# Four graph layers on one core: the last step and the tail in another order on TensorE, DVE and ACT

## The chip, the cores and the metric

The kernel runs on one core of a Trainium2 chip. The metric is the time of one execution in device microseconds, the median of several executions. The engines are named as in the profile: PE (TensorE, matmuls and transposes), DVE (VectorE), ACT (ScalarE), POOL (GpSimd) and SP (here only the queue of the loads and stores). Each engine works through its own list of instructions in order, and engines wait for each other by semaphores.

## The reference

The input is x, 32 graphs of 256 nodes with 128 features, and an adjacency matrix of 256 by 256. Four layers follow each other, each with a residual and a layer norm without weights over the 128 features:

```
x = layernorm(x + L0(x))   # A_hat x, Linear 128->256, batchnorm, relu, Linear 256->128, batchnorm
x = layernorm(x + L1(x))   # attention over 256 edges, 4 heads, softmax by source node, Linear
x = layernorm(x + L2(x))   # three layers S = adj*adj: relu(S x W1), relu(S h W2), S h W3 (128->256->512->128)
x = layernorm(x + L3(x))   # dense attention:
#   Wh = x W;  e = leaky_relu(Wh a1 + (Wh a2)^T);  e = -inf where adj == 0
#   L3 = softmax(e) Wh
```

Only the layers 2 and 3 are at work in the stretch that is changed.

## The kernel before

The 32 graphs are worked on in pairs, a pair is a **slot** (s = 0 or 1), and two slots are a **step** (p = 0 to 7, since `IT` is 8). The layers run as a pipeline over steps: while TensorE has layer 2 of step p in hand, layer 3 of step p - 2 and p - 1 is under way. All orders are written out by hand: each engine has a list of calls to small helper functions, and the order of these calls is the order of the work. There is no scheduler.

The names of the last steps are `K = IT - 3` (5), `M = IT - 2` (6) and `L = IT - 1` (7). When layer 2 of step L is being finished, layer 3 of K is finished beside it, and layer 3 of M and L is left for the tail. In the tail a piece of layer 3 is one slot and is numbered u: u = 0 and 1 are the slots of M, u = 2 and 3 those of L; j is the graph within the slot.

Layer 2 of step L, slot s, on its last stretch:

- `hidden2(L, s, g)` (PE, L1804): one of the four 128-row parts g of the projection to 512, as three matmuls for each product (a high and a low half of the numbers, L238 to L240). ACT applies the relu, `relu1` (L1541) for slot 1.
- `narrow(L, s)` (PE, L1811): the projection from 512 to 128. ACT rounds it, `s3_high` (L1402), DVE takes the rest, `s3_low` (L897), both out of PSUM.
- `mix_out(L, s)` (PE, L1822): the last product with the weighted adjacency. It needs `s3_low`.
- `add(L, s, ...)` (DVE, L875) adds the residual; `end_norm_stats(s)` (DVE, L1052), `end_power(s)` (POOL, L599) and `end_norm(s)` (DVE, L1065) are the layer norm behind it.

Layer 3 of a slot:

- `slot_scores(p, s, c, ...)` (DVE, L1044): Wh a1 or Wh a2 of four blocks of 128 nodes, c says which. c = 1 is what PE needs for `end_spread_scores(s)` (L1982), which lays the scores over the partitions.
- `end_maxima(s)` (DVE, L1074), `end_sums(s)` (ACT, L1492), `end_highest(s)` (DVE, L1082), `end_leaky(s)` (DVE, L1093), `end_exps(s)` (ACT, L1499): masked maximum, sum of both scores, leaky relu and exponential, in `soft`, which both steps M and L use. So L can't write slot s of `soft` before PE has turned the exponentials of M (`exr_done`, L1198 and L1209).
- `end_turn(u, s, j, base)` (PE, L1957), `end_copied` (ACT, L1509), `end_attend` (PE, L1965), `end_attended` (ACT, L1517), `end_output` (PE, L1974), `end_add` (DVE, L1100): transpose of the exponentials, the product with x, the product with W, division by the sum and residual.
- the norms that end layer 3: for K `ln_stats`, `ln_var_eps` (DVE, L178 and L192), `ln_power` (POOL, L200), `ln_scale` (ACT, L228) on the tile `ob`; for M the same for both slots at once, with slot 0 applied by DVE (`ln_apply`, L220) and slot 1 by ACT; for L by `fin_norm_stats`, `fin_power` and `fin_norm` (L1111, L604, L1125), a graph pair j at a time. SP stores K when `ln3.done` allows it, then graph by graph L slot 0, M, and L slot 1 (L398 to L407).

## Time and profile before

| | us |
|---|---|
| median of 3 runs | 585.36 |
| lowest and highest | 584.73 and 586.92 |
| the profiled execution | 586.41 |
| its span (first to last instruction) | 584.6 |
| PE, DVE, ACT, POOL busy | 537.5, 423.2, 370.3, 210.5 |
| mean granted share of TensorE's clock | 0.96 |

The span is what the instructions of the profiled execution cover, and 1.8 us lie around it. In a row of the timeline the first number is the start, the second how long the merged row lasts, and what stands in brackets is the idle time ahead of it and whose result ended it. The change touches only what starts after 534 us; the code up to there is the same.

### The profile page before, as it was taken

The numbers are of one execution on the slowest core, as the hardware profiler recorded it, in microseconds if no ns is written. First come the engines' busy times: TensorE is split into PE (matmuls) and PEld (weight loads), VectorE is DVE, ScalarE is ACT, GpSimd is POOL, SyncE is SP. The second block draws the span as 40 slices with busy tenths as digits, with TensorE's granted clock in tenths as the row PEclk, the third lists the DMA queues.
The fourth block names the chain that finished last, engine by engine and source line by source line (L and its number), as shares of the span: only waits on it lengthen the run. The fifth ranks groups of instructions, "written<-read, shape, count | busy, mean of one in ns | idle before, by whom it ended". The sixth has DMA issues, their size and how long they took to land.

```text
span 584.6 us, 11192 instructions
## 1 busy us (share of the span) xinstructions
PE 537.5 (92%) x3482; PEld 468.7 (80%) x3482; DVE 423.2 (72%) x1454; ACT 370.3 (63%) x741; POOL 210.5 (36%) x248
## 2 busy tenths in 40 slices
PE   3999799589999879999999999999999999999872
PEld 3888433468887679898998998998998998989762
DVE  4688667778986165358879679679778776787887
ACT  3666692557755414536568768778678677675682
POOL 8830530457575240501813513514514314310103
PEclk9999799689999769999999999999999999999997
DMA  7223000221200000000000100100100100100012
GB/s 229 72 79 101 2 0 0 72 74 44 64 0 1 0 2 1 1 0 2 2 1 2 36 0 1 36 0 0 36 0 0 36 1 0 38 0 1 2 37 73
DMA packets 28383, 15.26 MB, mean 26 GB/s; under 512 B 2320, under 2 KB 28048, under 8 KB 28352
## 3 DMA queue, kind: packets, MB, share of 16 engines
q1 hardware_dynamic: 27792, 13.65, 8.1%
q0 software_dynamic: 560, 1.25, 0.6%
q8 instruction: 14, 0.23, 0.2%
q14 instruction: 17, 0.14, 0.1%
HBM read 10.69 MB, written 4.19 MB: 25 GB/s over the span
## 4 chain that ended last, share of the span: by engine, by line
PE 79%; DVE 12%; ACT 4%; issue 2%; POOL 2%; DMA 0%; DVEq 0%; POOLq 0%; ACTq 0%; SPq 0%
PE psum L238 15%; PE psum L240 14%; PE psum L239 14%; PE psum L1818 9%; PE psum L1643 6%; PE psum L1685 5%; PE psum L1760 2%; PE psum L1770 2%; PE psum L1692 2%; PE psum L1696 2%; PE psum L1706 2%; DVE ln_st L184 2%; PE psum L1864 2%; PE psum L1846 2%; POOL ln_r L203 1%
## 5 line engine op out<-in xcount | busy, mean ns | idle before, releaser
L203 POOL TENSOR_TENSOR ln_r<-ln_v,mhalf 128x8 f32<-128x8 f32 x30 | 50.0, 1666 | 238.9 <-DVE ln_v L197 238.9
L1818 PE MATMUL psum<-l2w_s,h 128*128 128x128 f32 x512 | 59.8, 275 | 0.0
L1818 PEld LDWEIGHTS psum<-l2w_s,h 128*128 128x128 f32 x512 | 59.0, 192 | 0.8
L238 PE MATMUL psum<-qt_hi,l2w_s_hi 128*128 128x512 f32 x128 | 52.7, 412 | 0.0
L240 PE MATMUL psum<-qt_hi,l2w_s_lo 128*128 128x512 f32 x128 | 50.7, 396 | 0.0
L239 PE MATMUL psum<-qt_lo,l2w_s_hi 128*128 128x512 f32 x128 | 50.6, 395 | 0.0
L232 ACT ACTIVATE keep_x<-keep_x,ln_b,ln_r (+1 forms) x108 | 44.4, 487 | 7.0 <-DVE keep_x L224 4.4
L1400 ACT ACTIVATE h<-psum 128x512 f32<-128x512 f32 x60 | 34.8, 593 | 11.7 <-PE psum L240 11.6
L184 DVE BATCH_NORM_STATS2 ln_st<-keep_x 128x6 f32<-128x128 f32 (+1 forms) x192 | 39.4, 278 | 2.9 <-ACT keep_x L1328 1.6
L238 PE MATMUL psum<-wgt_hi,h_hi 128*128 128x256 f32 x128 | 37.1, 290 | 0.9 <-DVE h_lo L888 0.9
L240 PE MATMUL psum<-wgt_hi,h_lo 128*128 128x256 f32 x128 | 35.8, 280 | 0.0
L239 PE MATMUL psum<-wgt_lo,h_hi 128*128 128x256 f32 x128 | 35.7, 279 | 0.0
L1643 PE MATMUL psum<-hraw,w2t 128*128 (+1 forms) x64 | 32.1, 655 | 3.6 <-ACT hraw L1292 3.6
L1685 PE MATMUL psum<-sel,x1s_hi 128*128 128x512 f32 x64 | 27.6, 431 | 5.8 <-POOL x1s_lo L511 3.2
L888 DVE SCALAR_TENSOR_TENSOR h_lo<-psum,h_hi 128x1024 fp32r<-128x1024 f32 x16 | 19.6, 1225 | 16.2 <-ACT h_hi L1391 16.2
L1643 PEld LDWEIGHTS psum<-hraw,w2t 128*128 128x128 f32 x64 | 12.1, 207 | 22.9 <-issue 18.2
L911 DVE SCALAR_TENSOR_TENSOR soft<-keep_x,wa 128x128 f32<-128x128 f32 x96 | 30.0, 381 | 0.0
L899 DVE TENSOR_TENSOR s_lo<-psum,s_hi 128x512 fp32r<-128x512 f32 x16 | 11.1, 692 | 25.7 <-ACT s_hi L1404 25.7
L240 PEld LDWEIGHTS psum<-qt_hi,l2w_s_lo 128*128 128x128 f32 x128 | 24.1, 188 | 5.8
L1396 ACT ACTIVATE qt_hi<-psum 128x1024 fp32r<-128x1024 f32 x16 | 16.4, 1024 | 19.2 <-PE psum L240 19.2
L895 DVE TENSOR_TENSOR qt_lo<-psum,qt_hi 128x1024 fp32r<-128x1024 f32 x16 | 19.6, 1223 | 12.0 <-ACT qt_hi L1396 12.0
L239 PEld LDWEIGHTS psum<-qt_lo,l2w_s_hi 128*128 128x128 f32 x128 | 24.2, 189 | 4.4
(268 smaller groups left out, 1764.7 us busy)
## 6 DMA issues: line engine op xcount, KB each, us to landing
xin<-in_x SPq DMA_DIRECT2D x64, 128.0 KB, 2.3
out_x<-ob SPq DMA_DIRECT2D x24, 128.0 KB, 1.8
out_x<-keep_x SPq DMA_DIRECT2D x8, 128.0 KB, 1.9
l2w_raw<-in_l2w POOLq DMA_DIRECT2D x1, 512.0 KB, 5.1
adjs<-in_adj SPq DMA_DIRECT2D x1, 256.0 KB, 2.7
adjs<-in_adj_t SPq DMA_DIRECT2D x1, 256.0 KB, 2.9
l2w_s<-in_l2w POOLq DMA_DIRECT2D x1, 256.0 KB, 4.9
w_raw<-in_w_t SPq DMA_DIRECT2D x1, 128.0 KB, 2.8
```

Source lines behind the costliest of these rows:

```text
L184: i = dve.bn_stats(ln.st[:, s, k, :], y(s, k // 2, k % 2))
L203: pool.tensor_tensor(ln.r[:].rearrange("p s k -> p (s k)"), ln.v[:].rearrange("p s k -> p (s k)"), mhalf[:], ALU.pow).then_inc(ln.root, 1)
L232: i = act.activation(y(s, k // 2, k % 2), y(s, k // 2, k % 2), ACT.Identity, bias=ln.b[:, s, k:k + 1], scale=ln.r[:, s, k:k + 1])
L238: pe.matmul(o, lhs[0], rhs[0], start=start, stop=False)
L239: pe.matmul(o, lhs[0], rhs[1], start=False, stop=False)
L240: return pe.matmul(o, lhs[1], rhs[0], start=False, stop=stop)
L888: dve.scalar_tensor_tensor(out=h1[1][:, s].rearrange("p j t f -> p (j t f)"), in0=bank(2 * s, 2).rearrange("p k c -> p (k c)"), scalar=0.0 ...
L911: i = dve.scalar_tensor_tensor(out=soft[:, s, k, c * D:(c + 1) * D], in0=xn[:, q, k // 2, k % 2, :], scalar=1.0, in1=wa[:, c, :], op0=ALU. ...
L1400: act.activation(h2[:, s, g, :], bank(4 + g)[:, 0, :], ACT.Relu).then_inc(h2_out, 1)
L1643: i = pe.matmul(bank(s)[:, 0, :], w2t[:, k, :], hraw[:, k, q, :], start=(k == 0), stop=(k == 1))
L1685: i = pe.matmul(gathered_bank(s)[:, j, :], x1s[h][:, s, t, j, :], sel[:, t].rearrange("p k e -> p (k e)"), start=(n == 0), stop=(n == 3))
L1818: i = pe.matmul(bank(s)[:, 0, k * D:(k + 1) * D], h2[:, s, g, j * N + t * P:j * N + (t + 1) * P], l2w3_s[:, g, :], start=(g == 0), stop=(g ...
```

## The change

On **PE**, in the last step, the turn order becomes: `attend3(K, 1)`, `narrow(L, 0)`, `output3(K, 1)`, then both last projections to 512, `hidden2(L, 1, 0)` and `hidden2(L, 1, 1)`, then `mix_out(L, 0)` and `narrow(L, 1)`. The transposes of both slots of M stand behind `narrow(L, 1)`, and `mix_out(L, 1)` follows. In the tail the exponentials of L are turned later: slot 0's behind the outputs of M, and slot 1's in two halves around the product of slot 0.

On **DVE**, `s3_low(L, 0)` moves behind `slot_sum3(K, 1)`, the statistics of K are taken slot by slot, `s3_low(L, 1)` moves ahead of the scores of L's slot 0, and `add(L, 1)` with its norm moves ahead of `end_maxima(0)`. The norm of M is taken by slots (`end_norm_stats(2 + s)`), each behind that slot's additions, and DVE applies none of it.

On **ACT**, `s3_high(L, 0)` moves behind the exponentials of M's slot 0, the scaling of K's slots moves from between `end_copied(2, j)` and `end_sums(1)` to both sides of `s3_high(L, 1)`, the exponentials of L are split by halves, and both slots of M are scaled at the end.

On **POOL**, one power of eight numbers for M becomes two of four, each with its product.

```diff
@@ POOL
+            def sixth_shift(s):
+                pool.wait_ge(ln0.rstd, IT + 2 + s + 1)
+                pool.tensor_tensor(ln0.b[:, s], ln0.m[:, s], ln0.r[:, s], ALU.mult).then_inc(ln0.root, 1)
...
-            ln_power(pool, IT - 2, ln3)
+            for s in range(2):
+                end_power(2 + s)
+                sixth_shift(s)
@@ DVE
-            def end_norm_stats(s):
-                dve.wait_ge(ln2.added, 2 * L + s + 1)
+            def end_norm_stats(n):
+                s = n % 2
+                q = 2 * L + s if n < 2 else 2 * M + s
...
+                if n >= 2:
+                    dve.tensor_scalar(ln0.m[:, s], ln0.ag[:, s, :, 0], -1.0, None, ALU.mult)
...
-            s3_low(L, 0)
+            fifth_stats(0)
             leaky3(M, 1)
             slot_sum3(K, 1)
-            ln_stats(dve, last_sum, K, ln3)
+            s3_low(L, 0)
+            fifth_stats(1)
+            fifth_moments()
             ln_var_eps(dve, K, ln3)
             add(L, 0, o2_done, 2, ln2)
             end_norm_stats(0)
             weights3(M, False)
             end_norm(0)
+            s3_low(L, 1)
 
             dve.wait_ge(exr_done, 2 * M + 2)
             slot_scores(L, 0, 1, s12_ok)
-            s3_low(L, 1)
             slot_scores(L, 0, 0, own_ok)
-            end_maxima(0)
             add(L, 1, o2_done, 3, ln2)
             end_norm_stats(1)
+            end_maxima(0)
+            end_norm(1)
+
+            dve.wait_ge(exr_done, 2 * M + 4)
+            slot_scores(L, 1, 1, s12_ok)
             end_highest(0)
             end_leaky(0)
-            end_norm(1)
-
-            dve.wait_ge(exr_done, 2 * M + 4)
-            slot_scores(L, 1, 1, s12_ok)
             slot_scores(L, 1, 0, own_ok)
             end_maxima(1)
             end_highest(1)
...
                     end_add(M, s, j, 6 - 2 * s, ri, ln3.added if j else None)
-            ln_stats(dve, row(M), M, ln3)
-            ln_var_eps(dve, M, ln3)
+                end_norm_stats(2 + s)
...
                 fin_norm(0, j)
-            ln_apply(dve, row(M), lambda t, j: row(M)(0, t, j), M, 0, ln3)
@@ ACT
-            for s in range(2):
-                slot_sums(M, s)
+            slot_sums(M, 0)
+            attended(K, 1)
+            slot_sums(M, 1)
+            exps(M, 0)
             s3_high(L, 0)
-            attended(K, 1)
             relu1(0, 3)
-            exps(M, 0)
             relu1(1, 4)
             exps(M, 1)
+            ln_scale(act, last_sum, K, 0, ln3)
             s3_high(L, 1)
             for u, base in ((0, 6), (1, 4)):
                 for j in range(2):
                     end_copied(u, j, base)
+            ln_scale(act, last_sum, K, 1, ln3)
+            for j in range(2):
+                end_attended(0, j, 6)
             end_sums(0)
             for j in range(2):
-                end_attended(0, j, 6)
-            end_exps(0)
-            for j in range(2):
                 end_attended(1, j, 4)
+            end_exps(0, 0)
+            end_exps(0, 1)
+            end_sums(1)
+            end_exps(1, 0)
             for j in range(2):
                 end_copied(2, j, 2)
-            ln_scale(act, last_sum, K, 0, ln3)
-            ln_scale(act, last_sum, K, 1, ln3)
-            end_sums(1)
+            end_exps(1, 1)
             for j in range(2):
                 end_attended(2, j, 2)
-            end_exps(1)
...
-            act.wait_ge(ln3.done, 2 * M + 1)
-            ln_scale(act, row(M), M, 1, ln3)
+            for s in range(2):
+                act.wait_ge(ln0.root, IT + s + 1)
+                for k in range(4):
+                    y = row(M)(s, k // 2, k % 2)
+                    i = act.activation(y, y, ACT.Identity, bias=ln0.b[:, s, k:k + 1], scale=ln0.r[:, s, k:k + 1])
+                i.then_inc(ln3.done, 1)
@@ PE
             output3(K, 0)
+            attend3(K, 1)
             narrow(L, 0)
-            attend3(K, 1)
+            output3(K, 1)
             pe.wait_ge(tm_done, 2 * M + 1)
             hidden2(L, 1, 0)
-            output3(K, 1)
-            mix_out(L, 0)
             pe.wait_ge(tm_done, 2 * M + 2)
             hidden2(L, 1, 1)
-
-            pe.wait_ge(h2_out, GB * (2 * L + 1) + 2)
-            pe.wait_ge(ex_ready, 2 * M + 1)
-            for j in range(2):
-                end_turn(0, 0, j, 6)
+            mix_out(L, 0)
+
+            pe.wait_ge(ln3.added, 2 * K + 1)
+            narrow(L, 1)
+            for u, base in ((0, 6), (1, 4)):
+                pe.wait_ge(ex_ready, 2 * M + u + 1)
+                for j in range(2):
+                    end_turn(u, u, j, base)
 
             pe.wait_ge(ln3.added, 2 * K + 2)
-            narrow(L, 1)
+            mix_out(L, 1)
             end_spread_scores(0)
-            pe.wait_ge(ex_ready, 2 * M + 2)
-            for j in range(2):
-                end_turn(1, 1, j, 4)
-            mix_out(L, 1)
             for u, base in ((0, 6), (1, 4)):
                 for j in range(2):
                     end_attend(u, j, base)
             for j in range(2):
                 end_output(0, j, 6)
-            for j in range(2):
-                pe.wait_ge(ex_ready, 2 * L + j + 1)
-                end_turn(2, 0, j, 2)
             end_spread_scores(1)
             for j in range(2):
                 end_output(1, j, 4)
             for j in range(2):
+                pe.wait_ge(ex_ready, 2 * L + j + 1)
+                end_turn(2, 0, j, 2)
+            pe.wait_ge(ex_ready, 2 * L + 3)
+            end_turn(3, 1, 0, 0)
+            for j in range(2):
                 end_attend(2, j, 2)
+            pe.wait_ge(ex_ready, 2 * L + 4)
+            end_turn(3, 1, 1, 0)
...
-            for j in range(2):
-                pe.wait_ge(ex_ready, 2 * L + 2 + j + 1)
-                end_turn(3, 1, j, 0)
```

How DVE's instructions stand behind the addition of L's slot 0. `keep_x` is the stored x, `soft,s` and `wv,s` are the scores of c = 1 and c = 0, `s_lo` is `s3_low(L, 1)`, the ISA rows are the masked maxima. Before:

```order
L879 TENSOR_TENSOR keep_x<-psum,keep_x 128x512
L1056 BN_STATS ln_st<-keep_x 128x6 x4
L1060 BN_AGGR ln_ag<-ln_st 128x2 x4
L1063 TENSOR_SCALAR ln_v<-ln_ag 128x4
L955 RECIPROCAL ri<-rs 128x8
L1070 TENSOR_SCALAR keep_x<-keep_x,ln_ag,ln_r 128x128 x4
L1048 SCALAR_TENSOR_TENSOR soft,s<-keep_x,wa 128x128 x4
L899 TENSOR_TENSOR s_lo<-psum,s_hi 128x512
L1048 SCALAR_TENSOR_TENSOR wv,s<-keep_x,wa 128x128 x4
L1078 ISA soft,m<-psum,mask 128x256
L1078 ISA m 128x1
```

And after:

```order
L887 TENSOR_TENSOR keep_x<-psum,keep_x 128x512
L1069 BN_STATS ln_st<-keep_x 128x6 x4
L1073 BN_AGGR ln_ag<-ln_st 128x2 x4
L1078 TENSOR_SCALAR ln_v<-ln_ag 128x4
L963 RECIPROCAL ri<-rs 128x8
L1100 TENSOR_SCALAR keep_x<-keep_x,ln_ag,ln_r 128x128 x4
L907 TENSOR_TENSOR s_lo<-psum,s_hi 128x512
L1056 SCALAR_TENSOR_TENSOR soft,s<-keep_x,wa 128x128 x4
L1056 SCALAR_TENSOR_TENSOR wv,s<-keep_x,wa 128x128 x4
L887 TENSOR_TENSOR keep_x<-psum,keep_x 128x512
L1069 BN_STATS ln_st<-keep_x 128x6 x4
```

`s_lo` stands one group earlier, and the second addition follows the scores directly instead of the maxima.

How ACT's instructions stand in the tail, from the rounding of the last projection on. `s_hi` is `s3_high(L, 1)`, `h` is `end_copied`, `axt` is `end_attended`, `ob` is the scaling of K, `soft<-soft,s` are the sums and `soft,rs` the exponentials. Before:

```order
L1404 ACTIVATE s_hi<-psum 128x512
L1515 ACTIVATE h<-psum 128x512 x4
L1497 ACTIVATE soft<-soft,s 128x256 x4
L1520 ACTIVATE axt<-psum 128x256 x2
L1504 ACTIVATE soft,rs<-soft,zm 128x256 x4
L1520 ACTIVATE axt<-psum 128x256 x2
L1515 ACTIVATE h<-psum 128x512 x2
L232 ACTIVATE ob<-ob,ln_b,ln_r 128x128 x8
L1497 ACTIVATE soft<-soft,s 128x256 x4
L1520 ACTIVATE axt<-psum 128x256 x2
L1504 ACTIVATE soft,rs<-soft,zm 128x256 x4
```

And after:

```order
L232 ACTIVATE ob<-ob,ln_b,ln_r 128x128 x4
L1434 ACTIVATE s_hi<-psum 128x512
L1545 ACTIVATE h<-psum 128x512 x4
L232 ACTIVATE ob<-ob,ln_b,ln_r 128x128 x4
L1550 ACTIVATE axt<-psum 128x256 x2
L1527 ACTIVATE soft<-soft,s 128x256 x4
L1550 ACTIVATE axt<-psum 128x256 x2
L1535 ACTIVATE soft,rs<-soft,zm 128x256 x4
L1527 ACTIVATE soft<-soft,s 128x256 x4
L1535 ACTIVATE soft,rs<-soft,zm 128x256 x2
L1545 ACTIVATE h<-psum 128x512 x2
L1535 ACTIVATE soft,rs<-soft,zm 128x256 x2
```

The eight scalings of K no longer stand ahead of the second group of sums; four of them stand ahead of `s_hi` instead, and four behind the copies of M.

How DVE's instructions stand behind the last leaky relu, where the additions and the norm of M are. `keep_x<-psum,ri,keep_x` are the additions of M, those with `ri_last` the additions of L. Before:

```order
L1106 SCALAR_TENSOR_TENSOR keep_x<-psum,ri,keep_x 128x128 x8
L184 BN_STATS ln_st<-keep_x 128x6 x8
L189 BN_AGGR ln_ag<-ln_st 128x2 x8
L195 TENSOR_SCALAR ln_m<-ln_ag 128x8
L197 TENSOR_SCALAR ln_v<-ln_ag 128x8
L1225 RECIPROCAL ri_last<-rs 128x4
```

And after:

```order
L1136 SCALAR_TENSOR_TENSOR keep_x<-psum,ri,keep_x 128x128 x4
L1069 BN_STATS ln_st<-keep_x 128x6 x4
L1073 BN_AGGR ln_ag<-ln_st 128x2 x4
L1077 TENSOR_SCALAR ln_m<-ln_ag 128x4
L1078 TENSOR_SCALAR ln_v<-ln_ag 128x4
L1136 SCALAR_TENSOR_TENSOR keep_x<-psum,ri,keep_x 128x128 x4
```

The group of the norm has half the width and stands twice, once for each slot.

## Rows read from the trace of the kernel before

**Rows 1.** The page, the chain that ended last, share of the span by engine.

```profile
PE 79%; DVE 12%; ACT 4%; issue 2%; POOL 2%; DMA 0%; DVEq 0%; POOLq 0%; ACTq 0%; SPq 0%
```

**Rows 2.** Timeline of PE, last step and tail: start, us, engine, line, count, [idle before].

```profile
544.19 0.39 PE L238 MATMUL psum<-qt_hi,l2w_s_hi 128*128 128x512 f32 x1
...
545.58 1.04 PE L1961 MATMUL psum<-ident,soft 128*128 128x128 f32 x8
546.52 3.81 PE L1818 MATMUL psum<-l2w_s,h 128*128 128x128 f32 x32
552.46 0.65 PE L1988 MATMUL psum<-ident,s 128*128 128x128 f32 x4 [2.12 <-DVE soft L1048]
...
553.74 0.37 PE L238 MATMUL psum<-s_hi,wgt_hi 128*128 128x256 f32 x1
...
555.20 1.02 PE L1970 MATMUL psum<-h,keep_x 128*128 128x256 f32 x4
```

**Rows 3.** Timeline of DVE from the last step to the last leaky relu.

```profile
543.08 1.13 DVE L1143 SCALAR_TENSOR_TENSOR ob<-psum,ri,keep_x 128x128 f32<-128x128 f32 x4 [1.38 <-PE psum L1864]
...
546.99 0.68 DVE L879 TENSOR_TENSOR keep_x<-psum,keep_x 128x512 f32<-128x512 f32 x1
...
550.31 1.11 DVE L1070 TENSOR_SCALAR keep_x<-keep_x,ln_ag,ln_r 128x128 f32<-128x128 f32 x4 [1.01 <-POOL ln_r L602]
551.46 0.29 DVE L1048 SCALAR_TENSOR_TENSOR soft<-keep_x,wa 128x128 f32<-128x128 f32 x1
...
552.32 0.69 DVE L899 TENSOR_TENSOR s_lo<-psum,s_hi 128x512 fp32r<-128x512 f32 x1
...
555.39 0.69 DVE L879 TENSOR_TENSOR keep_x<-psum,keep_x 128x512 f32<-128x512 f32 x1 [0.17 <-PE psum L240]
...
557.52 0.16 DVE L1086 TENSOR_TENSOR zm<-m,s 128x4 f32<-128x4 f32 x1
...
559.36 1.10 DVE L1070 TENSOR_SCALAR keep_x<-keep_x,ln_ag,ln_r 128x128 f32<-128x128 f32 x4
...
561.35 0.29 DVE L1048 SCALAR_TENSOR_TENSOR wv<-keep_x,wa 128x128 f32<-128x128 f32 x1
...
563.70 0.16 DVE L1086 TENSOR_TENSOR zm<-m,s 128x4 f32<-128x4 f32 x1
...
565.60 1.62 DVE L1098 SCALAR_TENSOR_TENSOR soft<-soft 128x256 f32<-128x256 f32 x4 [1.33 <-ACT soft L1497]
```

**Rows 4.** Timeline of DVE, the tail behind the last leaky relu.

```profile
567.14 2.15 DVE L1106 SCALAR_TENSOR_TENSOR keep_x<-psum,ri,keep_x 128x128 f32<-128x128 f32 x8
...
571.97 0.17 DVE L1225 RECIPROCAL ri_last<-rs 128x4 f32<-128x4 f32 x1
...
576.64 1.11 DVE L224 TENSOR_SCALAR keep_x<-keep_x,ln_ag,ln_r 128x128 f32<-128x128 f32 x4
577.66 0.61 DVE L1106 SCALAR_TENSOR_TENSOR keep_x<-psum,ri_last,keep_x 128x128 f32<-128x128 f32 x2
```

**Rows 5.** Timeline of ACT in the last step and the tail.

```profile
535.28 3.29 ACT L1489 ACTIVATE soft<-soft,s 128x256 f32<-128x256 f32 x8
...
550.37 0.60 ACT L1404 ACTIVATE s_hi<-psum 128x512 fp32r<-128x512 f32 x1 [2.03 <-PE psum L1818]
...
561.99 3.18 ACT L232 ACTIVATE ob<-ob,ln_b,ln_r 128x128 f32<-128x128 f32 x8
```

**Rows 6.** Timeline of POOL: the power of the norm of L's slot 0.

```profile
549.27 1.01 POOL L602 TENSOR_TENSOR ln_r<-ln_v,mhalf 128x4 f32<-128x4 f32 x1 [0.20 <-DVE ln_v L1063]
```

**Rows 7.** Timeline of PE in the tail, as in group 2.

```profile
567.08 1.16 PE L1978 MATMUL psum<-l3w_s,axt 128*128 128x128 f32 x8 [2.32 <-ACT axt L1520]
...
568.34 2.10 PE L1961 MATMUL psum<-ident,soft 128*128 128x128 f32 x8
570.23 2.70 PE L1970 MATMUL psum<-h,keep_x 128*128 128x256 f32 x8
```

**Rows 8.** Windows: stretch, length, PE busy, granted clock (PEclk), DMA share, GB/s.

```profile
568.60:571.70 3.10, 3.10 (x12) 0.50 0.00 0
```

More of the change, by code:

```diff
@@ L597, in _, with end_power @@
             step(IT - 2, two_ahead=False)
-            def end_power(s):
-                pool.wait_ge(ln0.var, IT + s + 1)
+            def end_power(n):
+                s = n % 2
+                pool.wait_ge(ln0.var, IT + n + 1)
                 pool.tensor_tensor(ln0.r[:, s], ln0.v[:, s], mhalf[:, 0:4], ALU.pow).then_inc(ln0.rstd, 1)
+            def sixth_shift(s):
+                pool.wait_ge(ln0.rstd, IT + 2 + s + 1)
+                pool.tensor_tensor(ln0.b[:, s], ln0.m[:, s], ln0.r[:, s], ALU.mult).then_inc(ln0.root, 1)
             def fin_power(s, j):
@@ L1050, in slot_scores @@
                 i.then_inc(ok, 1)
-            def end_norm_stats(s):
-                dve.wait_ge(ln2.added, 2 * L + s + 1)
+            def end_norm_stats(n):
+                s = n % 2
+                q = 2 * L + s if n < 2 else 2 * M + s
+                if n < 2:
+                    dve.wait_ge(ln2.added, 2 * L + s + 1)
+                else:
+                    dve.wait_ge(ln3.added, 2 * M + s + 1)
                 for k in range(4):
-                    i = dve.bn_stats(ln0.st[:, s, k, :], xn[:, 2 * L + s, k // 2, k % 2, :])
+                    i = dve.bn_stats(ln0.st[:, s, k, :], xn[:, q, k // 2, k % 2, :])
                 i.then_inc(ln0.stats, 1)
-                dve.wait_ge(ln0.stats, 2 * IT + s + 1)
+                dve.wait_ge(ln0.stats, 2 * IT + n + 1)
                 for k in range(4):
@@ L1061, in end_norm_stats, with fifth_stats, fifth_moments @@
                 i.then_inc(ln0.mean, 1)
-                dve.wait_ge(ln0.mean, IT + s + 1)
+                dve.wait_ge(ln0.mean, IT + n + 1)
+                if n >= 2:
+                    dve.tensor_scalar(ln0.m[:, s], ln0.ag[:, s, :, 0], -1.0, None, ALU.mult)
                 dve.tensor_scalar(ln0.v[:, s], ln0.ag[:, s, :, 1], LN_EPS, None, ALU.add).then_inc(ln0.var, 1)
+            def fifth_stats(s):
+                dve.wait_ge(ln3.added, 2 * K + s + 1)
+                for k in range(4):
+                    i = dve.bn_stats(ln3.st[:, s, k, :], ob[:, s, k // 2, k % 2, :])
+                i.then_inc(ln3.stats, 1)
+            def fifth_moments():
+                dve.wait_ge(ln3.stats, 2 * K + 2)
+                for s in range(2):
+                    for k in range(4):
+                        i = dve.bn_aggr(ln3.ag[:, s, k, :], ln3.st[:, s, k, :])
+                i.then_inc(ln3.mean, 1)
             def end_norm(s):
@@ L1196, in _ @@
             end_norm(0)
+            s3_low(L, 1)
             dve.wait_ge(exr_done, 2 * M + 2)
             slot_scores(L, 0, 1, s12_ok)
-            s3_low(L, 1)
             slot_scores(L, 0, 0, own_ok)
-            end_maxima(0)
             add(L, 1, o2_done, 3, ln2)
             end_norm_stats(1)
-            end_highest(0)
-            end_leaky(0)
+            end_maxima(0)
             end_norm(1)
@@ L1210, in _ @@
             slot_scores(L, 1, 1, s12_ok)
+            end_highest(0)
+            end_leaky(0)
             slot_scores(L, 1, 0, own_ok)
@@ L1497, in end_sums, with end_exps @@
                     act.activation(soft[:, s, k, :], soft[:, s, k, :], ACT.Identity, bias=s12[:, s, 0, k:k + 1]).then_inc(zt_ready, 1)
-            def end_exps(s):
+            def end_exps(s, j):
                 act.wait_ge(m_step, 3 * L + 3 * s + 3)
-                for n, k in enumerate(L3_ORDER):
+                for n in (2 * j, 2 * j + 1):
+                    k = L3_ORDER[n]
                     act.wait_ge(lk_ready, 2 * L + 4 * s + n + 1)
@@ L1505, in end_exps @@
                                        accum_out=rs[:, s, k:k + 1])
-                    if n % 2:
-                        i.then_inc(ex_ready, 1)
+                i.then_inc(ex_ready, 1)
             def end_copied(u, j, base):
@@ L1578, in _ @@
                 end_attended(3, j, 0)
-            act.wait_ge(ln3.done, 2 * M + 1)
-            ln_scale(act, row(M), M, 1, ln3)
+            for s in range(2):
+                act.wait_ge(ln0.root, IT + s + 1)
+                for k in range(4):
+                    y = row(M)(s, k // 2, k % 2)
+                    i = act.activation(y, y, ACT.Identity, bias=ln0.b[:, s, k:k + 1], scale=ln0.r[:, s, k:k + 1])
+                i.then_inc(ln3.done, 1)
         @block.tensor
```

## The prediction, made before the changed kernel ran

> **What bounds the kernel now.** I first read the chain that ended last: PE carries 79% of it, DVE 12%, ACT 4% [rows 1]. That is an average. The change touches only the last 50 us, so I went on to the timelines of that stretch, engine by engine, and asked at each wait what came last.
>
> Until 545.58 PE has no gap: the last projection to 512 (six matmuls from 544.19 to 545.58, so 1.39 for each `hidden2`) and the turns behind it follow each other [rows 2]. Then PE narrows slot 1, waits 2.12 us for DVE's scores, and starts `mix_out(L, 1)` only at 553.74 [rows 2]. It waits because DVE is late: the addition of L's slot 0 starts at 546.99, its norm waits for POOL, and `s3_low(L, 1)`, without which `mix_out(L, 1)` can't start, comes at 552.32 behind the scores [rows 3]. ACT had its half ready at 550.97 [rows 5].
>
> From the second addition (555.39) on, DVE is the bound. Its one idle time is 1.33 us ahead of the last leaky relu at 565.60 [rows 3]: ACT, which owes it the sums, has just scaled both slots of K for 3.18 us [rows 5]. The four pieces of that relu then start 0.4 apart, as ACT delivers, and DVE reaches the additions of M at 567.14 [rows 3, 4]. Behind it DVE works nearly without a gap to the end: additions and norm of M until 571.97, half of the norm of M from 576.64 to 577.66, the second slot of L from 577.66 [rows 4]. So the question is when the second addition starts, what DVE has to do from there to 567.14, and what behind it.
>
> **Part 1: up to the addition of L's slot 0.** The list of PE up to and with `mix_out(L, 0)` holds the same work in another order, and PE had no gap, so it is through at 545.58 again; `mix_out(L, 0)` takes 1.46 (553.74 to 555.20) and starts at 544.12 [rows 2]. DVE's additions start 0.19 behind the end of PE's piece (555.20 to 555.39) [rows 2, 3], so this one starts at 545.77 instead of 546.99. It is no longer late, since the statistics of K begin earlier by slots.
>
> This adds a wait: `mix_out(L, 0)` now needs `s3_low(L, 0)`, which stands behind `slot_sum3(K, 1)` on DVE, and that behind `output3(K, 1)`. Output3 is through two hidden2 ahead of 544.12, at 541.34. The sum of K takes 1.13 [rows 3], the low part 0.69 [rows 3], with some 0.3 for handoffs: 543.5. On ACT, `slot_sums(M, 0)` ends at 536.9 (half of 3.29 behind 535.28 [rows 5]), and with one copy, four more sums, four exponentials (each at most 0.5 us) and `s3_high` it is through at 541.9. So the wait is covered by 0.6 us. Behind that wait on PE stands everything else, so this cover is the place where it can fail.
>
> **Part 2: to the second addition.** From 545.77: POOL's power starts 2.28 behind the addition (546.99 to 549.27) at 548.05, DVE's norm 1.04 behind that (549.27 to 550.31) at 549.09, takes 1.15, and `s3_low(L, 1)` runs from 550.24 to 550.93 [rows 3, 6]. PE is there at the same time: narrowing, which now has no turns ahead of it, starts at 545.58; it lasts 3.81 to the last result, and `s3_high` follows 3.85 behind its start (546.52 to 550.37) [rows 2, 5], so 549.43 to 550.03, ahead of the 550.24. Sixteen turns take 1.9 (0.94 for eight) and PE is free at 551.0 [rows 2]. `mix_out(L, 1)` starts at 551.0, the addition 1.65 later (553.74 to 555.39) at 552.65 [rows 2, 3]. DVE has done both groups of scores by then (0.86 each, 550.93 to 552.65) [rows 3]. Before it was 555.39: **2.74 us earlier**. ACT's scaling of K's slot 0 now stands ahead of `s3_high(L, 1)`. It needs POOL's power of K; DVE's moments of K are through at 545.1, before addition 0, the power some 2 us later, and half of 3.18 gives 548.7 [rows 5]: hidden by 0.7 us.
>
> **Part 3: DVE from the second addition to the additions of M.** Before: 555.39 to 567.14, 11.75 us [rows 3, 4]. After, DVE has in a row: addition and statistics 2.13 (555.39 to 557.52), maxima of slot 0, norm and first scores 2.01 (550.31 to 552.32), highest and leaky 1.84 (557.52 to 559.36), scores and maxima of slot 1 2.35 (561.35 to 563.70), highest and leaky again 1.84; the maxima alone are 2.35 less 0.86, 1.49 [rows 3]. Sum 11.66. The maxima are moved into this stretch (+1.49), and the idle 1.33 and the stretched relu (0.2) go out of it. The sums on ACT stand right behind the exponentials now, start when the last maxima come and end about 0.1 before DVE's relu asks for them. So the additions of M start at 552.65 + 11.66 = 564.31 instead of 567.14: **2.83 us earlier**.
>
> **Part 4: the tail.** Additions and norm of M took 4.83 (567.14 to 571.97) [rows 4]. By slots each has four additions, 1.08 (half of 2.15 [rows 4]) with 0.04 for the handoff, and statistics, 1.44 (2.13 less the 0.69 of the addition [rows 3]) with one more small operation of 0.06 to 0.16: 2.62, twice 5.24, **0.41 more**. DVE no longer applies slot 0 of M (576.64 to 577.66): **1.02 less** [rows 4]. ACT takes it (half of 3.18, 1.6), behind its last copies, when nothing but the stores of M waits for it, which lie ahead of the last store. POOL does two powers of 1.01 [rows 6] where it is idle.
>
> **Sum.** -2.83 + 0.41 - 1.02 = -3.44 us. Against the profiled execution, 586.41, that is 583.0. That execution lay 1.05 above the median of the runs, 585.36, and against the median it is **581.9 us**.
>
> **What PE's tail may cost.** PE does the last part (turn, product, output of u = 2 and 3) beside DVE's additions. DVE wants the output of u = 2 at 564.31 + 5.24, 569.6, and of u = 3 at 574.2 (577.66 less 571.97, less 1.02, behind it [rows 4]). PE can turn slot 1's first half about when DVE's additions of M start, at 564.3, and by my count waits for that for some 2.8 us. At full clock what is left takes half of the 11.1 us of rival A, 5.6, and with some 0.7 of waits for ACT's copies it ends at 570.6, the output of u = 2 near 567.8: 1.8 and 3.6 us of cover. The clock is open: before, PE waited 2.32 us up to 567.08 and from 568.60 to 571.70 the granted clock was 0.50, 1.2 GHz, and eight turns took 2.10 instead of 1.04, the products 2.70 [rows 2, 7, 8]. The wait of 2.12 us ahead of 552.46 brought no such fall. One low stretch as long costs at most 1.7 us of PE, inside the cover: 0 to 0.2 us. The bound from the other side is rival A.
>
> The Trainium skill ("TensorE: Matmul & The Clock Gate", section "HAM oscillation — how this bites in real kernels") says that idle gaps between bursts of matmuls put the clock to half, and that it takes busy time to come back. [...]
>
> **Rival A: the clock stays at half from 564.3 to the end of PE's work.** PE has 8 turns (1.9), 16 product passes (0.34 each, a part of the 2.70 for eight, 5.4) and 16 output passes (0.24 as the turns, 3.8) [rows 7], 11.1 with waits to 12.3, so output 3 comes about 576.1 instead of being wanted at 574.2: 1.9 us of the gain go, 583.8. For it: the longer gap and the sparse work before it. Against: in the trace the low stretch lasted 3.1 us and ended while PE was still at it [rows 8].
>
> **Rival B: the handoffs eat the gain.** Three covers are thin: 0.6 (`s3_low(L, 0)`), 0.7 (scaling of K ahead of `s3_high(L, 1)`), 0.1 (sums ahead of the relu). If each fails by 0.5 us the gain is 3.4 less 1.5, and the time 583.5; if only the tail's 0.6 remains, 584.8.
>
> **Rival C, slower: `mix_out(L, 0)` waits, and the clock falls in the last step.** Behind this wait on PE stand narrowing, 16 turns, `mix_out(L, 1)`: 3.5 + 1.9 + 1.46 = 6.9 us at full clock [rows 2]. If ACT's `s3_high(L, 0)` behind the exponentials, or DVE's sum of K, makes PE wait long enough that the clock goes to 0.50 there, this takes 6.9 us more, of which all but about 0.1 reaches the second addition: 581.9 + 6.9 = 588.8. Without a fall of the clock it is slower from a wait of 3.4 us on, with one from any wait that brings it. Against it: 2.32 us is the shortest wait here ahead of a fall [rows 7], and with the 0.6 of cover the two halves would have to come 2.9 us later than counted in Part 1.
>
> **That it doesn't do what it says**: if the gap ahead of `mix_out(L, 1)` is refilled by DVE's own delay and nothing moves, only the tail's -0.6 is left, within rival B.
>
> **Chances.** Forecast 0.64 (gain 2.6 to 4), rival A 0.13, rival B 0.18, rival C 0.05. The range that holds 8 in 10 is 581.3 to 584.6: it takes in A and most of B. Faster by over 0.5%, which is 2.9 us and about what a measurement can tell from no change, asks for 582.4 or less: most of the forecast's share, as it lies only 0.5 inside, so 0.55; within 0.5% 0.40; slower 0.05.
>
> **What would show it.** In the profile after, against the same start: `mix_out(L, 0)` without a wait and followed by the addition near 545.8; `mix_out(L, 1)` near 551.0 and the second addition near 552.7; no idle time of DVE ahead of the last leaky relu, additions of M near 564.4; norm of M in two groups, none applied by DVE; DVE not waiting for an output of PE. Wrong would be a wait of PE for `s_lo` in the last step, DVE waiting in the tail for what `end_output` writes, or a second addition later than 553.5.

## The result and the profile after

| | before | after |
|---|---|---|
| median of 5 runs, us | 586.58 | 581.31 |
| lowest to highest | 584.73 to 587.04 | 581.24 to 582.44 |
| the profiled execution, its span | 586.41, 584.6 | 581.25, 579.4 |
| mean granted share of TensorE's clock | 0.960 | 0.965 |

The ratio is 0.993 with a 95% interval of 0.9909 to 0.995: the changed kernel is 0.7% faster. I had forecast 3.44 us less in the profiled execution; it is 5.16 less, and the rows say where the 1.7 us on top come from. The median of 581.31 lies just inside the range that I gave (581.3 to 584.6), by 0.01 us.

To compare the last stretch of two executions I take one mark on DVE in both, the first small operation on the maxima of M (`zm`, L929 before), which stands ahead of all that is changed. It is at 534.73 before, and the last normalisation at 581.64:

```profile
534.73 0.17 DVE L929 TENSOR_TENSOR zm<-m,s 128x8 f32<-128x8 f32 x1
...
581.64 0.60 DVE L1131 TENSOR_SCALAR keep_x<-keep_x,ln_ag,ln_r 128x128 f32<-128x128 f32 x2 [0.33 <-POOL ln_r L607]
```

DVE's timeline in the changed kernel, with the same mark at its head:

```profile
533.14 0.17 DVE L937 TENSOR_TENSOR zm<-m,s 128x8 f32<-128x8 f32 x1
...
544.21 0.69 DVE L887 TENSOR_TENSOR keep_x<-psum,keep_x 128x512 f32<-128x512 f32 x1 [0.66 <-PE psum L240]
...
547.54 1.12 DVE L1100 TENSOR_SCALAR keep_x<-keep_x,ln_ag,ln_r 128x128 f32<-128x128 f32 x4 [1.01 <-POOL ln_r L603]
548.69 0.69 DVE L907 TENSOR_TENSOR s_lo<-psum,s_hi 128x512 fp32r<-128x512 f32 x1
...
551.18 0.69 DVE L887 TENSOR_TENSOR keep_x<-psum,keep_x 128x512 f32<-128x512 f32 x1
...
561.32 1.42 DVE L1128 SCALAR_TENSOR_TENSOR soft<-soft 128x256 f32<-128x256 f32 x4
562.66 1.12 DVE L1136 SCALAR_TENSOR_TENSOR keep_x<-psum,ri,keep_x 128x128 f32<-128x128 f32 x4
...
565.28 1.12 DVE L1136 SCALAR_TENSOR_TENSOR keep_x<-psum,ri,keep_x 128x128 f32<-128x128 f32 x4
...
567.90 0.17 DVE L1256 RECIPROCAL ri_last<-rs 128x4 f32<-128x4 f32 x1
568.11 0.61 DVE L1136 SCALAR_TENSOR_TENSOR keep_x<-psum,ri_last,keep_x 128x128 f32<-128x128 f32 x2
...
572.57 0.60 DVE L1136 SCALAR_TENSOR_TENSOR keep_x<-psum,ri_last,keep_x 128x128 f32<-128x128 f32 x2
...
576.53 0.60 DVE L1161 TENSOR_SCALAR keep_x<-keep_x,ln_ag,ln_r 128x128 f32<-128x128 f32 x2 [0.33 <-POOL ln_r L613]
```

The mark comes 1.59 us earlier, in a part of the program that is the same. From the mark to the last normalisation it is 43.39 us; before it was 46.91 (534.73 to 581.64): 3.52 less. I call this time **the stretch** from here on. The wait of 1.33 us ahead of the leaky relu [rows 3] is gone, and its four pieces follow each other without a gap (1.42 instead of 1.62). From the second addition on DVE has only one wait, at the very end, for POOL. Where DVE's share of the norm of M stood for 1.02 us [rows 4], the additions of L's slot 1 now follow directly (572.57).

PE in the changed kernel, with the same columns as in [rows 2]:

```profile
542.59 0.28 PE L238 MATMUL psum<-s_hi,wgt_hi 128*128 128x256 f32 x1
...
544.00 3.74 PE L1854 MATMUL psum<-l2w_s,h 128*128 128x128 f32 x32
547.58 1.91 PE L1997 MATMUL psum<-ident,soft 128*128 128x128 f32 x16
549.53 0.36 PE L238 MATMUL psum<-s_hi,wgt_hi 128*128 128x256 f32 x1
```

From the last projections to 551 PE has no wait: the 2.12 us in [rows 2] are gone, and the first mixing (542.59), narrowing, 16 turns and the second mixing (549.53) follow each other. In the tail:

```profile
562.97 1.00 PE L1997 MATMUL psum<-ident,soft 128*128 128x128 f32 x4 [2.52 <-ACT soft L1535]
...
567.31 1.06 PE L2014 MATMUL psum<-l3w_s,axt 128*128 128x128 f32 x8
```

and the granted clock there, in three stretches with the columns of [rows 8]:

```profile
561.50:563.00 1.50, 0.03 (x1) 1.00 0.00 0
563.20:566.60 3.40, 3.40 (x11) 0.51 0.03 7
566.70:571.00 4.30, 4.27 (x29) 1.00 0.00 0
```

PE waited 2.52 us, and from 0.2 us behind the end of that wait it worked for 3.4 us at half clock. Before, it was the same behind 2.32 us of waiting [rows 7, 8]. The output of slot 2 began at 567.31 and DVE fetched it at 568.11 without waiting.

### The profile page after: what moved, and what is told of

Read it like the earlier page. It is cut to its first block, busy times and chain, and to the rows that moved or that the text cites. A ratio compares the mean times of both kernels' runs of the same rounds, so it can differ in the third digit from the quotient of the medians.

```text
span 579.4 us, 11193 instructions
## 1 busy us (share of the span) xinstructions
PE 534.2 (92%) x3482; PEld 466.6 (81%) x3482; DVE 421.5 (73%) x1452; ACT 372.0 (64%) x745; POOL 210.8 (36%) x250
## 3 DMA queue, kind: packets, MB, share of 16 engines
HBM read 10.69 MB, written 4.19 MB: 26 GB/s over the span
## 4 chain that ended last, share of the span: by engine, by line
PE 79%; DVE 11%; POOL 3%; issue 2%; ACT 2%; DMA 1%; SPq 1%; DVEq 0%; POOLq 0%; ACTq 0%
PE psum L238 14%; PE psum L240 14%; PE psum L239 14%; PE psum L1854 9%; PE psum L1679 5%; PE psum L1721 5%; PE psum L1796 2%; PE psum L1806 2%; PE psum L1728 2%; PE psum L1732 2%; PE psum L1742 2%; PE psum L1900 2%; PE psum L1882 2%; DVE ln_st L184 1%; POOL ln_r L203 1%
## 5 line engine op out<-in xcount | busy, mean ns | idle before, releaser
L203 POOL TENSOR_TENSOR ln_r<-ln_v,mhalf 128x8 f32<-128x8 f32 x29 | 48.3, 1667 | 222.8 <-DVE ln_v L197 222.8
L232 ACT ACTIVATE keep_x<-keep_x,ln_b,ln_r (+1 forms) x104 | 42.7, 487 | 2.6 <-POOL ln_b L206 2.6
L184 DVE BATCH_NORM_STATS2 ln_st<-keep_x 128x6 f32<-128x128 f32 (+1 forms) x184 | 37.7, 279 | 2.8 <-ACT keep_x L1358 1.7
```

The costliest lines, as they stand in the source:

```text
L184: i = dve.bn_stats(ln.st[:, s, k, :], y(s, k // 2, k % 2))
L203: pool.tensor_tensor(ln.r[:].rearrange("p s k -> p (s k)"), ln.v[:].rearrange("p s k -> p (s k)"), mhalf[:], ALU.pow).then_inc(ln.root, 1)
L232: i = act.activation(y(s, k // 2, k % 2), y(s, k // 2, k % 2), ACT.Identity, bias=ln.b[:, s, k:k + 1], scale=ln.r[:, s, k:k + 1])
```

## The experiments

All kernels are measured by the stretch of one profiled execution, in which the start has no part; where the total matters, several executions follow. Offsets "from the mark" are differences of two rows. The code cuts leave lines out at `...`. All the stretches, in us:

| kernel | mark | last normalisation | stretch |
|---|---|---|---|
| before | 534.73 | 581.64 | 46.91 |
| changed | 533.14 | 576.53 | 43.39 |
| norm_once | 534.94 | 579.33 | 44.39 |
| norm_slots_alone | 534.41 | 580.73 | 46.32 |
| low_behind_scores | 534.07 | 578.38 | 44.31 |
| turns_ahead | 534.09 | 578.16 | 44.07 |
| scale_late | 532.97 | 579.12 | 46.15 |
| high_late | 535.29 | 581.61 | 46.32 |
| after_filled | 531.47 | 574.86 | 43.39 |
| before_filled | 531.40 | 578.29 | 46.89 |
| after_again | 533.33 | 576.72 | 43.39 |
| act_norm | 535.07 | 577.41 | 42.34 |
| act_norm_early | 534.03 | 576.35 | 42.32 |
| act_norm_early_filled | 533.11 | 575.42 | 42.31 |

Where kernels have the same last part, the stretch agrees within 0.03 us, while the mark lies anywhere between 531.40 and 535.29.

**1. The norm of M at once again (norm_once).**

```diff
-                end_norm_stats(2 + s)
+            ln_stats(dve, row(M), M, ln3)
+            ln_var_eps(dve, M, ln3)
...
+            ln_apply(dve, row(M), lambda t, j: row(M)(0, t, j), M, 0, ln3)
```

> The changed kernel with the norm of M as before: both slots at once, slot 0 applied by DVE. The stretch is read from DVE's first small sum of M's maxima (zm) to its last normalisation; it was 46.91 us before and is 43.39 in the changed kernel. Theory (the tail is DVE's own work): DVE gets 1.02 back for applying slot 0 and saves 0.41, so the stretch is 43.39 + 0.6 = 44.0 us, all of it behind the additions of M, whose start does not move. Rival (the gain of the tail comes from PE or ACT, the norm's place is indifferent): 43.4 us.

Measured: stretch 44.39, so 1.00 more, not 0.6. DVE's timeline there:

```profile
569.31 0.17 DVE L1255 RECIPROCAL ri_last<-rs 128x4 f32<-128x4 f32 x1
569.87 0.61 DVE L1134 SCALAR_TENSOR_TENSOR keep_x<-psum,ri_last,keep_x 128x128 f32<-128x128 f32 x2 [0.39 <-PE psum L2010]
...
574.33 1.11 DVE L224 TENSOR_SCALAR keep_x<-keep_x,ln_ag,ln_r 128x128 f32<-128x128 f32 x4
```

The norm at once is 0.41 shorter, as counted (564.48 to 569.31 is 4.83, against 5.24), so the reciprocal comes 34.37 from the mark (569.31 less 534.94) instead of 34.76. But then DVE waits 0.39 for PE's output, and the additions of L start 34.93 from the mark instead of 34.97. So in the new order the longer norm by slots lies in a wait for PE and costs nothing, and taking the 1.02 us of applying off DVE counts in full.

**2. The norm by slots alone, in the kernel before (norm_slots_alone).**

```diff
-            ln_stats(dve, row(M), M, ln3)
-            ln_var_eps(dve, M, ln3)
+                end_norm_stats(2 + s)
...
-            ln_apply(dve, row(M), lambda t, j: row(M)(0, t, j), M, 0, ln3)
```

> The kernel before with one part of the change alone: the norm of M by slots, both applied by ACT. Theory: the parts add up and this one is worth 0.6, so the stretch is 46.91 - 0.6 = 46.3 us, the rest of the gain (2.9) needs the new order. Rival (the additions of M are held by a wait and a shorter DVE tail only waits for PE, whose low clock stands in this tail): 46.9 us, with an idle time of DVE ahead of L's slot 1.

Measured: stretch 46.32, 0.59 less than before, as expected. In this order PE's output is ready in time, DVE does not wait, and the 0.41 is paid:

```profile
566.85 1.12 DVE L1121 SCALAR_TENSOR_TENSOR keep_x<-psum,ri,keep_x 128x128 f32<-128x128 f32 x4
...
569.47 1.12 DVE L1121 SCALAR_TENSOR_TENSOR keep_x<-psum,ri,keep_x 128x128 f32<-128x128 f32 x4
...
572.30 0.61 DVE L1121 SCALAR_TENSOR_TENSOR keep_x<-psum,ri_last,keep_x 128x128 f32<-128x128 f32 x2
```

566.85 to 572.30 is 5.45, against 5.04 before, from 567.14 [rows 4] to 572.18:

```profile
572.18 0.61 DVE L1106 SCALAR_TENSOR_TENSOR keep_x<-psum,ri_last,keep_x 128x128 f32<-128x128 f32 x2
```

The total shows nothing of it: ratio 0.9998, interval 0.998 to 1.0015 over 10 executions. An effect of 0.6 us is below what the totals of this kernel can tell; the profile tells it.

**3. The low part behind the scores again (low_behind_scores).**

```diff
-            s3_low(L, 1)
-
             dve.wait_ge(exr_done, 2 * M + 2)
             slot_scores(L, 0, 1, s12_ok)
+            s3_low(L, 1)
```

> The changed kernel with one line back: the low part of the last narrowing behind the first scores of L's slot 0 again, not ahead of them. Theory (the low part sets when PE can mix slot 1, and that sets the second addition): PE waits 0.9 us ahead of the last mixing, the second addition comes 0.88 later and the stretch is 43.39 + 0.88 = 44.3 us. Rival (PE's turns set it, the low part is hidden behind them, since both come within 0.1 us of each other): 43.4 us.

Measured: stretch 44.31, 0.92 more, where 0.88 was expected. PE waits, and the second addition with it, 18.96 from the mark instead of 18.04:

```profile
551.34 0.36 PE L238 MATMUL psum<-s_hi,wgt_hi 128*128 128x256 f32 x1 [0.93 <-DVE s_lo L907]
```

One line of DVE's order is a quarter of the gain.

**4. The turns of slot 0 ahead of the narrowing again (turns_ahead).**

```diff
-            narrow(L, 1)
             for u, base in ((0, 6), (1, 4)):
...
+                if u == 0:
+                    narrow(L, 1)
```

> The changed kernel with the turns of M's slot 0 ahead of the last narrowing again, those of slot 1 behind it. Theory: the narrowing comes 0.94 later, ACT's high part with it (0.2 of cover), PE waits 0.7 ahead of the last mixing, which follows by 0.7, and the stretch is 43.39 + 0.65 to 0.7 = 44.1 us. Rival (the order of turns and narrowing does nothing, all 16 turns and the narrowing are done before the mixing either way): 43.4 us.

Measured: stretch 44.07, 0.68 more, as expected. Now DVE waits for ACT's high part, which comes 0.87 later (549.59 less 534.09 is 15.50 from the mark, against 14.64), 0.18 of which were covered:

```profile
550.29 0.69 DVE L907 TENSOR_TENSOR s_lo<-psum,s_hi 128x512 fp32r<-128x512 f32 x1 [0.69 <-ACT s_hi L1434]
```

Both edits of the prediction's second part are needed: with either one taken back PE waits ahead of the second mixing. No run takes both back at once, so what they are worth together isn't measured.

**5. ACT's scaling of K late again (scale_late).**

```diff
-            ln_scale(act, last_sum, K, 0, ln3)
             s3_high(L, 1)
...
             end_exps(0, 1)
+            for s in range(2):
+                ln_scale(act, last_sum, K, s, ln3)
             end_sums(1)
```

> The changed kernel with ACT's scaling of both slots of K back where it was, ahead of the last group of sums. Theory (ACT's 3.2 us of scaling, not the sums themselves, made DVE wait 1.33 us before): DVE waits 1.9 us ahead of its last leaky relu, the pieces of the relu then start 0.4 apart, the additions of M come 2.1 later and the stretch from zm to the last normalisation is 43.39 + 2.1 = 45.5 us. Rival (DVE alone sets the tail, ACT has slack enough): 43.4 us.

Measured: stretch 46.15, so 2.76 more, where 2.1 was expected.

```profile
563.11 1.62 DVE L1128 SCALAR_TENSOR_TENSOR soft<-soft 128x256 f32<-128x256 f32 x4 [1.85 <-ACT soft L1527]
564.64 1.12 DVE L1136 SCALAR_TENSOR_TENSOR keep_x<-psum,ri,keep_x 128x128 f32<-128x128 f32 x4
...
570.69 0.61 DVE L1136 SCALAR_TENSOR_TENSOR keep_x<-psum,ri_last,keep_x 128x128 f32<-128x128 f32 x2 [0.63 <-PE psum L2014]
```

The wait ahead of the relu is 1.85, the additions of M come 31.67 from the mark, 2.15 later. The rest, 0.63, is a wait for PE. PE had waited 5.00 us for the exponentials, up to 565.31, 2.51 later from the mark than in the changed kernel (32.34 instead of 29.83), and the clock was at half for 6.8 us, from within that wait on:

```profile
562.80:569.50 6.70, 4.19 (x12) 0.51 0.21 62
```

PE worked for 4.19 us at half clock, against 3.40 in the changed kernel, which costs it 0.4 us by my estimate (half of the difference). About as much comes from the wait itself: PE begins 2.51 later and DVE's additions only 2.15. So this is a part of my rival A and not all of it: the fall is longer, but the clock is whole again ahead of the end of PE's work.

**6. A wait of PE in the last step (high_late).**

```diff
             exps(M, 0)
-            s3_high(L, 0)
             relu1(0, 3)
             relu1(1, 4)
+            s3_high(L, 0)
```

> The changed kernel with ACT's high part of the first narrowing moved behind both relus of the last projections, so that PE has to wait ahead of the first mixing. It measures the cover of that place (rival C of the prediction). Theory: the high part comes 3.7 later, 1.6 of it are covered, PE waits 2.1, everything behind moves by 2.1, the clock stays at 1.00 through the last narrowing, and the stretch is 43.39 + 2.1 = 45.5 us. Rival (a wait of this length brings the clock down for narrowing, turns and mixing): 3 to 7 us more than that, 48.5 or later.

Measured: stretch 46.32, 2.93 more, where 2.1 was expected. PE waits 1.90 ahead of the first mixing, the additions of L and M come 2.16 to 2.17 later, and from the mixing to the tail the clock stays whole. In the tail it falls for 6.8 us, from within PE's wait on, and DVE waits for PE once more:

```profile
546.00:565.00 19.00, 16.25 (x120) 1.00 0.10 28
565.60:572.40 6.80, 5.11 (x16) 0.50 0.01 4
```

```profile
573.18 0.61 DVE L1136 SCALAR_TENSOR_TENSOR keep_x<-psum,ri_last,keep_x 128x128 f32<-128x128 f32 x2 [0.79 <-PE psum L2014]
```

So a wait of 1.90 us in the midst of dense work did not bring the clock down, and rival C at its full price did not come. With the same 2.52 us of waiting in the tail as in the changed kernel (up to 567.29) the fall was twice as long, and PE worked for 5.11 us in it instead of 3.40. That is the part of the 2.93 that my expectation lacked.

**7. PE kept busy in its wait for the first batchnorm (after_filled, before_filled).** The same edit in the changed kernel and in the kernel before:

```diff
+            for _ in range(28):
+                pe.transpose(bank(1)[:, 0, 0:P], ident[:], ident[:])
             pass2(0, True)
```

> The changed kernel with 28 transposes of the identity (3.1 us at full clock, result unused) put into PE's wait of 3.5 us for the first batchnorm, ahead of the second linear layer. There the profiled execution of before had a granted clock of 0.50 for 6.8 us, that of the changed kernel for 3.4 us, which by itself is 1.7 us of difference. Theory (the 1.7 us by which the changed kernel gained more than its last 50 us explain come from this stretch, by the luck of a run): with PE kept busy the clock does not fall there, zm comes at 531.4 instead of 533.14, the runs lie at 579.6, and they scatter less than the 3 us of the kernel before. The stretch stays 43.39. Rival (the clock falls anyway, or the second layer waits for ACT's relu and does not feel it): zm at 533 to 535, 581 to 583 us.

> The kernel before with the 28 transposes in PE's wait for the first batchnorm. Theory: its start is then that of the filled changed kernel, zm at 533.1 less 0 (534.73 less 3.3 for the 6.8 us of half clock, and 1.6 of it given back because the transposes end 0 to 0.3 later than the wait): 531.4 to 531.8, stretch 46.91, total 579.6 + 3.5 = 583.1 us, and the filled pair differs by 3.5 us, 0.6%, which is the change alone. Rival: the filled pair still differs by 5 us, and the change also speeds up the start.

Measured: the mark at 531.47 in the one and 531.40 in the other, stretches 43.39 and 46.89. Medians 579.57 (4 executions) and 583.06 (10): 3.49 us, 0.6%, between the filled pair. The two were measured on different chips, where the median of the unfilled kernel before was 585.76 and 586.49. Against it, the ratios are 0.9898 (0.9881 to 0.9915) and 0.9953 (0.9936 to 0.9969); by these the pair differs by 0.55%, 3.2 us. So the totals bear out 3.5 us roughly, and the agreement of 3.49 with the stretches is luck. The second linear layer on PE in four kernels, all 64 matmuls of it merged: before, changed,

```profile
67.73 32.14 PE L1643 MATMUL psum<-hraw,w2t 128*128 128x512 f32 x64 [3.56 <-ACT hraw L1292]
```

```profile
68.06 31.05 PE L1679 MATMUL psum<-hraw,w2t 128*128 128x512 f32 x64 [3.54 <-ACT hraw L1322]
```

changed and filled, before and filled:

```profile
64.30 3.25 PE L1683 MATMUL psum<-ident 128*128 128x128 f32 x28
68.01 29.38 PE L1679 MATMUL psum<-hraw,w2t 128*128 128x512 f32 x64 [0.45 <-ACT hraw L1322]
```

```profile
64.03 3.25 PE L1647 MATMUL psum<-ident 128*128 128x128 f32 x28
67.90 29.38 PE L1643 MATMUL psum<-hraw,w2t 128*128 128x512 f32 x64 [0.62 <-ACT hraw L1292]
```

The granted clock explains it: PE worked for 5.7 us of the fall before and for 3.4 us in the changed kernel, and half of that is 2.9 and 1.7 us, against 2.76 and 1.67 measured. Before, and in the changed kernel, at the head of that layer:

```profile
66.90:73.70 6.80, 5.97 (x8) 0.52 0.00 0
```

```profile
68.20:71.60 3.40, 3.40 (x5) 0.50 0.00 0
```

Filled, it is 1.00 there. So at this place the start loses 1.7 to 2.8 us to the clock, the edit takes that away in both kernels, and with marks 0.07 us apart the change has no part in it. My expectation of less scatter failed: the filled kernel before still ran from 581.15 to 584.69.

Later falls differ too. Apart from those in the tail, all falls lie ahead of 221 us. In the kernel before there are five, of 37.5 us in all, and PE worked for 32.2 us in them. In the changed kernel the second, near 105 us, also lasted 3.4 us instead of 6.8, and PE worked for 26.9 us in all five. In the five profiles with 23.7 to 26.9 us of such work the mark is at 531.40 to 533.14, in the nine with 30.3 to 32.9 us at 533.33 to 535.29.

**8. The changed kernel again (after_again).**

> The changed kernel once more, on the chip that runs the other kernels of this group. Theory (the change is worth the 3.5 us of its last stretch, and the 1.6 us on top were the start of those runs): stretch 43.39, median 582.0 to 582.5 beside a before of about 585.8. Rival (the start is faster for good, whatever causes it): 581.3 again, zm near 533.1.

Measured: median 582.39 of 5, ratio 0.9941 (0.992 to 0.9962), stretch 43.39. The mark was at 533.33. The stretch is the same to the hundredth, while the median is 1.08 us above the first one. It was another chip, and the two profiled executions differ by only 0.19 us at the mark, so what made the median move isn't shown.

**9. One norm more on ACT (act_norm, act_norm_early, act_norm_early_filled).** DVE bounds the tail, so ACT applies the last norm of L's slot 0:

```diff
@@ DVE
-            for j in range(2):
-                fin_norm(0, j)
@@ ACT, at the end
+            for j in range(2):
+                act.wait_ge(ln1.root, IT + j + 1)
+                for t in range(T):
+                    k = 2 * t + j
+                    y = row(L)(0, t, j)
+                    i = act.activation(y, y, ACT.Identity, bias=ln1.b[:, 0, k:k + 1], scale=ln1.r[:, 0, k:k + 1])
+                i.then_inc(ln0.done, 1)
```

Left out here are the waits of the stores, the small operation on DVE that gives the negative mean and POOL's product with it.

> The changed kernel with the last norm of L's slot 0 applied by ACT instead of DVE, with one more small operation on DVE and one on POOL for each half. Theory (DVE bounds the tail, ACT is idle there): DVE is rid of 1.21 us and pays 0.16, the stretch is 43.39 - 1.05 = 42.3 us. Rival (with DVE faster, PE's outputs of L's slot 1 or ACT's last scaling and the stores end last): 43.0 us or more, with DVE waiting for PE ahead of the additions of L's slot 1.

Measured: stretch 42.34, as expected, and yet nothing won: the median is 583.54 (ratio 0.9965, 0.9951 to 0.9978), above the changed kernel. DVE, and ACT beside it:

```profile
577.41 0.60 DVE L1166 TENSOR_SCALAR keep_x<-keep_x,ln_ag,ln_r 128x128 f32<-128x128 f32 x2 [0.33 <-POOL ln_r L613]
```

```profile
574.41 0.88 ACT L1619 ACTIVATE keep_x<-keep_x,ln_b,ln_r 128x128 f32<-128x128 f32 x2 [0.71 <-POOL ln_b L616]
575.19 3.17 ACT L1625 ACTIVATE keep_x<-keep_x,ln_b,ln_r 128x128 f32<-128x128 f32 x8
```

DVE ends at 578.01, the span at 582.9, 4.9 later; in the changed kernel it was 2.3 (577.13 to 579.4). ACT's scaling of M now stands behind the norm of L and ends at 578.36, and SP issues in the order of its list: two stores of M's last slot and, behind them, two of L's last slot, 128 KB each, have to wait for it. From the mark to the end of the span it is 47.9 us instead of 46.3. The second try puts the scaling of M's slot 0 ahead of the last two copies of PE's products, that of slot 1 right behind them, and the stores of M ahead of those of L:

> The changed kernel with the last norm of L's slot 0 on ACT, and ACT's scaling of M earlier: slot 0 ahead of the last copies of PE's products, slot 1 right behind them, and the stores of M ahead of those of L. In the first try DVE's stretch fell to 42.34, but the end of the span lay 4.9 us behind DVE's last normalisation instead of 2.3, because M's last scaling and four stores stood at the end. Theory: DVE's stretch stays at 42.3, and the span ends 2.3 to 2.4 us behind DVE's end again, so 1.05 us ahead of the changed kernel. Rival (PE's output of L's slot 1 comes late, since the scaling delays its copy): stretch 42.8 or more, with DVE waiting for PE.

> The version above with the 28 transposes in PE's wait for the first batchnorm. Theory: both gains add up, zm at 531.5, stretch 42.3, total 579.6 - 1.05 = 578.5 us, 1.2% below the kernel before. Rival (the two share a cover): 579.5 us.

Measured: stretch 42.32, DVE ends at 576.95 and the span at 579.5, and ACT's timeline is

```profile
569.19 1.64 ACT L1617 ACTIVATE keep_x<-keep_x,ln_b,ln_r 128x128 f32<-128x128 f32 x4
570.73 0.67 ACT L1553 ACTIVATE axt<-psum 128x256 f32<-128x256 f32 x2
571.29 1.63 ACT L1617 ACTIVATE keep_x<-keep_x,ln_b,ln_r 128x128 f32<-128x128 f32 x4
572.83 1.64 ACT L1629 ACTIVATE keep_x<-keep_x,ln_b,ln_r 128x128 f32<-128x128 f32 x4
```

From the mark to the end of the span it is 45.5 us against 46.3, so 0.9 less, where 1.05 was expected. With the 28 transposes the median of 6 is 579.59 (577.14 to 580.55), ratio 0.9878 (0.9856 to 0.9901), against 579.57 of the filled changed kernel without it; 578.5 was expected, and 579.5 was the rival's. The mark of that profiled execution was at 533.11, not 531.5, with its first fall at 102.6 us, so the start was another one; the stretch was 42.31. The 0.9 us show in the profile and not in the totals, whose ratios (0.9878 and 0.9898) have intervals that overlap. A version that beats both kernels exists, the filled changed one at 0.9898; that the norm on ACT adds to it is shown in the stretch only.

## Why the prediction was right

The direction, the mechanism and the size of the change came out. The profiled execution fell by 1.7 us more than forecast, of which 1.6 us lie in the start, outside the change. That the median still came into the range, by 0.01 us, is luck; in the second measurement of the same kernel it was 582.39. Taken by its own steps, with my times moved by the 1.59 us of the mark:

| step | predicted | measured |
|---|---|---|
| first mixing starts | 542.53 | 542.59 |
| first addition | 544.18 | 544.21 |
| second mixing | 549.41 | 549.53 |
| second addition | 551.06 | 551.18 |
| additions of M | 562.72 | 562.66 |
| additions and norm of M | 5.24 | 5.24 (562.66 to 567.90) |
| from the mark to the last normalisation | -3.44 | -3.52 |

**Part 1** held: the added wait of PE for `s3_low(L, 0)` was covered (PE has no gap at 542.59), and the first addition comes 11.07 from the mark instead of 12.26. Experiment 6 measures the cover on ACT's side: the high part came 3.7 us later by the order and PE waited 1.90, so 1.8 us were covered. The thinner cover, 0.6 us by my count for DVE's sum of K and the low part, no run used up: the low part ends at 541.82, 0.77 ahead of the mixing. No run takes the order of this part back by itself, so its share of the 3.52 isn't measured alone.

**Part 2** held, and experiments 3 and 4 show that it is two edits with the same cover: 0.92 and 0.68 us come back when either goes.

**Part 3** held. DVE's sum was 11.66 us, measured 11.48 (551.18 to 562.66); most of the difference is in the maxima of slot 0, 1.37 instead of 1.49. Experiment 5 shows the cause of the 1.33: with ACT's 3.2 us of scaling back in their place the wait is there again, as 1.85.

**Part 4** had the right sum and one wrong cover. I charged 0.41 for the norm by slots, which experiment 2 confirms in the kernel before, and expected DVE to be 1.8 us behind PE's output at full clock, so that every 0.41 of DVE's would count. With the fall of the clock that I had named, PE's output was just in time, and without the norm by slots DVE would have waited 0.39 (experiment 1). In the changed kernel the norm by slots is free and its part of the gain is 1.00, not 0.61; the new order alone gives 2.52 of the 3.52.

**The clock** did what one of my two bounds said: one fall of 3.4 us behind a wait of 2.52, where I had counted 2.8, costing DVE nothing. The 3.1 us that I had read before [rows 8] are a part of a fall of 3.4 us. A fall of twice that length came in experiments 5 and 6, where DVE waited 0.63 and 0.79 us for PE, in experiment 5 in part because PE began later. Rival A, half clock up to the end of PE's work for 1.9 us, came in no run.

**What I did not forecast** is the start. I took the median of three executions, 585.36, and subtracted the change. The start of the kernel is not one number: the mark was at 534.73 in one profile of before, 533.14 in that of the changed kernel, and from 532.97 to 535.29 over the nine unfilled ones after it. Of the 5.16 us between the two profiled executions 3.52 are the change, 1.59 the start, and 0.05 lie behind the last normalisation. The start goes with how much work PE does while the clock is at half (experiment 7); what decides that isn't shown.

## What to carry to other kernels

When an engine idles, look for what stands ahead of the late instruction in its releaser's own queue, and move that; two edits may share one cover, so judge them together and take each back alone. Work taken off the engine that bounds the end pays only if the queue it lands on, and the stores that wait behind it in order, end earlier than the bound. Compare profiles from a mark behind the unchanged part: it told 0.1 us here, while the median of one and the same kernel came out as 581.31 and as 582.39.
